# Gated delta layer of an eight-layer kernel: one table set for the norm, repeated identity products, and a new order around the key products

## The reference, cut to what matters

```
err = einsum('bhij,bhj->bhi', S, kt) - vt
S = at[..., None] * S - bt[..., None, None] * (err[..., None] * kt[:, :, None, :])
o = einsum('bhij,bhj->bhi', S, qt)
```

## Time and profile before

| | us |
|---|---|
| median of 3 runs | 2849.22 |
| lowest, highest | 2838.45, 2849.55 |
| the profiled execution's own time | 2847.4 |
| its span | 2845.6 |
| busy VectorE (DVE) | 2072.3 (73%) |
| busy ScalarE (ACT) | 1626.4 (57%) |
| busy TensorE products (PE), weight loads (PEld) | 2388.4 (84%), 1591.6 (56%) |
| mean granted TensorE clock, share of 2.4 GHz | 0.923 |

### The profile page before, as it was taken

How to read it: one execution, slowest core, us unless ns; L and a number is a source line. 1 busy time by engine, 2 the same in 40 slices (tenths; PEclk the granted TensorE clock), 3 DMA queues, 4 the chain that set the end, 5 groups by cost and what they waited for, 6 DMA issues and landing times. The chain is left out here.

```text
span 2845.6 us, 63751 instructions
## 1 busy us (share of the span) xinstructions
PE 2388.4 (84%) x25649; PEld 1591.6 (56%) x25701; DVE 2072.3 (73%) x3811; ACT 1626.4 (57%) x4119; POOL 263.7 (9%) x278
## 2 busy tenths in 40 slices
PE   6788888877888788887994999999997886999777
PEld 5666666666667666664442666666642322332376
DVE  6889998889889889882123777778726775886465
ACT  3656677666666766665234777777641113667344
POOL 0000000000000000000011101100002342110342
PEclk9889999889999989998996999999998998999889
DMA  5110111111011111002006999999510003231422
GB/s 185 32 32 17 32 32 32 32 32 30 19 32 32 32 32 30 19 17 71 0 12 173 236 249 227 232 241 233 127 37 0 0 0 103 54 88 24 172 71 65
DMA packets 205726, 219.48 MB, mean 77 GB/s; under 512 B 32966, under 2 KB 191446, under 8 KB 199990
## 3 DMA queue, kind: packets, MB, share of 16 engines
q1 hardware_dynamic: 203033, 210.44, 28.3%
q0 software_dynamic: 2400, 4.95, 0.5%
HBM read 137.96 MB, written 79.79 MB: 77 GB/s over the span
## 5 line engine op out<-in xcount | busy, mean ns | idle before, releaser
L2871 DVE TENSOR_REDUCE dl_ZO<-dl_XP 128x64 f32<-128x128 f32 (+6 forms) x448 | 219.7, 490 | 15.5
L1990 ACT ACTIVATE da_AB<-ps 128x384 f32<-128x384 f32 x256 | 124.7, 491 | 140.8 <-PE ps L1851 137.1
L2866 DVE TENSOR_TENSOR dl_XP<-dl_ZO,dl_G 128x128 f32<-128x128 f32 (+5 forms) x384 | 177.0, 461 | 13.2
L2000 ACT ACTIVATE da_E<-ps,da_top 128x512 f32<-128x512 f32 x256 | 176.2, 688 | 17.2 <-DVE da_top L2146 16.7
L2143 DVE TENSOR_TENSOR ps<-ps,da_window 128x192 f32<-128x192 f32 (+1 forms) x256 | 101.3, 396 | 116.3 <-PE ps L1874 112.0
L1470 DVE TENSOR_REDUCE ra_top<-ps 128x1 f32<-128x512 f32 x256 | 159.2, 680 | 36.2 <-PE ps L1236 22.8
L2146 DVE TENSOR_REDUCE da_top<-ps 128x1 f32<-128x512 f32 x256 | 176.9, 691 | 8.8
L2450 PE MATMUL ps<-dl_ST,ident 128*128 128x512 f32 x256 | 139.3, 672 | 46.0 <-ACT dl_Q L2638 46.0
L1370 ACT ACTIVATE ra_PT<-ps 128x512 f32<-128x512 f32 x256 | 136.0, 601 | 61.0 <-PE ps L1267 59.1
L1881 PE MATMUL ps<-ident,da_E 128*128 128x128 f32 x1024 | 168.7, 288 | 1.6 <-ACT da_E L2000 1.5
L2384 PEld LDWEIGHTS ps<-X,dl_taps_v 128*128 128x128 f32 x1088 | 145.5, 216 | 18.2 <-issue 12.9
(11 more groups left out here) (411 smaller groups left out, 5855.9 us busy)
## 6 DMA issues: line engine op xcount, KB each, us to landing
da_bands<-da_AB SPq DMA_DIRECT2D x128, 384.0 KB, 3.8
dl_Abc<-dl_ends SPq DMA_DIRECT2D x64, 512.0 KB, 6.2
da_window<-da_bands SPq DMA_DIRECT2D x128, 192.0 KB, 4.4
da_across<-da_bands SPq DMA_DIRECT2D x128, 192.0 KB, 4.5
da_parts<-da_split SPq DMA_DIRECT2D x64, 96.0 KB, 3.4
ra_parts<-ra_split SPq DMA_DIRECT2D x16, 384.0 KB, 3.5
rf_We<-in_rf_We SPq DMA_DIRECT2D x1, 4608.0 KB, 24.1
da_K<-da_parts SPq DMA_DIRECT2D x16, 256.0 KB
```

The lines of the kernel that those rows point to most:

```text
L1990: eng.activation(AB[:, j % STAGES, h, :, :], ps[:, band_bank(v), 0:2 * BAND].rearrange("p (k x) -> p k x", k=2), ACT.Copy)\
L2000: eng.activation(E[:, U % 2, :], ps[:, score_bank(U), :], ACT.Exp, bias=top[:, u:u + 1], accum_out=total[:, m % 2, u:u + 1]).then_inc(s["e ...
L2866: link(eng.tensor_tensor(XP[:, :, :, SB - t:], seen.unsqueeze(1).to_broadcast([P, 2, I, t + 1]), G[:, x:x + 2, keys][:, ::-1, :].unsqueeze ...
L2871: link(eng.tensor_reduce(ZO[:, to:to + 1 + (2 * I - 1) * CH:CH].rearrange("p (k i) -> p k i", k=2), XP[:, :, :, SB - 1 - t:], AXX, ALU.add))
```

## The change

Four edits, all in `delta_attention`:

1. ScalarE's `deviation` loads the set with both Ln and Exp by name before it waits for the variance, and the third eviction of pass n+1 goes behind it.
2. TensorE multiplies quarter 2 with the identity five times more, right before `kept(2)`, into the same bank with start and stop set, so that the following `kept(2)` overwrites it.
3. In `boundary(n, 1)` the last key products go behind the updates, and on VectorE `prepare(n + 1, 1)` goes ahead of `gate_keys(n + 1)` and the residual.
4. ScalarE's `lay_values(n + 1, 1)` is cut in two: steps 0 to 3, then the copy of the later products, then steps 4 to 15.

```diff
+    REPEATS = 5
...
-            def kept(r):
-                eng.matmul(ps[:, UPDATES[r], :], c.ident[:, :], quarters[:, r, :, :], start=True, stop=False)
+            def kept(r, alone=False):
+                eng.matmul(ps[:, UPDATES[r], :], c.ident[:, :], quarters[:, r, :, :], start=True, stop=alone)
...
                 eng.sem_inc(c.past, 1)
+                for g, k, h, r in itertools.product(range(GR), range(2), range(2), range(GR)):
+                    update(g, k, h, r)
                 if e == 1:
                     key_products(LAST_KEYS).then_inc(s["g"], 1)
-                for g, k, h, r in itertools.product(range(GR), range(2), range(2), range(GR)):
-                    update(g, k, h, r)
...
                 eng.wait_ge(s["evac"], (n + 1) * PROJ + 3)
+                for _ in range(REPEATS):
+                    kept(2, True)
                 kept(2)
...
             def deviation(n):
+                eng.preload_act_table_set("natural_log_exp_and_others")
                 eng.wait_ge(s["var"], n + 1)
...
-            def lay_values(m, e):
+            def lay_values(m, e, first=0, last=CH):
...
-                for t in range(CH):
+                for t in range(first, last):
                     ins = eng.activation(bv[:, e, :, t], values[:, t, :], ACT.Copy, scale=beta_now[:, 0, t:t + 1])
-                ins.then_inc(s["laid"], 1)
+                if last == CH:
+                    ins.then_inc(s["laid"], 1)
...
-                evacuate(n + 1, 1, 3)
+                evacuate(n + 1, 1, 2)
                 if not first:
                     deviation(n - 1)
+                evacuate(n + 1, 2, 3)
...
-                lay_values(n + 1, 1)
+                lay_values(n + 1, 1, 0, 4)
                 later_products(n + 1)
+                lay_values(n + 1, 1, 4)
                 scale_decays(n + 1, 1)
...
                 end(n, 1, first)
+                prepare(n + 1, 1)
                 gate_keys(n + 1)
                 if not first:
                     residual(n - 1)
-                prepare(n + 1, 1)
                 begin(n + 1, 0)
```

## The result

| | before | after |
|---|---|---|
| median, us | 2850.22 (6 runs) | 2863.73 (6 runs, 2859.57 to 2868.29) |
| profiled execution, its span | 2847.4, 2845.6 | 2868.29, 2866.5 |
| busy VectorE | 2072.3 | 2072.8 |
| busy ScalarE | 1626.4 | 1583.3 |
| busy TensorE products | 2388.4 | 2426.2 |

The kernel before was measured again beside the changed one. The ratio of the runs is 1.0049, with a 95% interval of 1.0030 to 1.0068: the changed kernel is 14 us slower. The forecast was 2865. The time was forecast well, but two of its terms were off in opposite directions, so part of the agreement is luck; the steps are taken one by one further down.

What follows compares the result with a forecast made beforehand. VectorE was taken to bound the stage, through its waits before L2803 (new starts) and L2831 (cross products). +6 for the first two edits and +12 for the last two made +18 on 2847.4, so 2865 us, range 2826 to 2882.

Steps and rivals of the forecast that it cites:

- What bounds the kernel: VectorE sets the stage's period, standing still before L2803 for new starts (67.0 us) and L2831 for cross products (12.6 us).
- (a): TensorE no longer waits at L2450 for the logarithm, which follows the variance product directly, with one table load before it.
- (b): In first halves TensorE runs 18 kept-product records in a row (8.1 us), with transposes some 2 us behind W.
- (c): VectorE's wait for new starts before L2803 in second halves is under 1 us in most passes.
- (d): ScalarE stands idle 2 to 4 us before L2612, the copy of the later products.
- (e): VectorE's wait for cross products before L2831 is near 3 us a pass, some 45 us in all, against 12.6.
- +6: First and second edit, us over 15 passes: per pass -3.07 for the wait, +4.5 for repeats, -0.9 for the clock.
- +12: Third and fourth edit together, us: VectorE's waits at L2803 and L2831 go from 2.9 to 3.65 a pass, times 16.
- Rival 1: Later products come early as TensorE's issue stalls fall elsewhere, clock as forecast: -19, 2828 us; chance 0.17.
- Rival 2: TensorE is granted 2.4 GHz through first halves, second halves as forecast: -6, 2841 us; chance 0.15.
- Rival 3: Gate keys come late, so VectorE waits before L2747, and repeats run partly at 1.2 GHz: 2881 us; chance 0.10.
- Rival 4: The wait before L2803 shrinks by what L2831's grows, and repeats fill idle time: 2849 us; chance 0.14.

Runs made afterwards that it cites:

- norm_rep: The kernel before with only the first and second edit: 2859.88 us against 2865.28 for the kernel before, ratio 0.9990.
- nosplit: The changed kernel with the fourth edit undone, all 16 value scalings ahead of the later products' copy: 2825.99 us against 2852.01 for the kernel before, ratio 0.9913.
- split_only: The kernel before with the fourth edit alone: 2904.57 us against 2865.95 for the kernel before, ratio 1.0133.
- split12: The whole change, but twelve value scalings ahead of the later products' copy and four behind: 2847.13 us against 2868.03 for the kernel before, ratio 0.9922.
- rep3: The changed kernel without its fourth edit and with three repeated identity products, not five: 2819.47 us against 2865.28 for the kernel before, ratio 0.9853.
- rep1: The changed kernel without its fourth edit and with one repeated identity product, not five: 2822.82 us against 2865.28 for the kernel before, ratio 0.9863.
- rep2: The changed kernel without its fourth edit and with two repeated identity products, not five: 2821.92 us against 2865.95 for the kernel before, ratio 0.9852.

## Right or wrong, step by step

- **What bounds the kernel** held throughout. Every experiment's mark follows VectorE's idle time, most of it in the two waits and, where the third edit is in, in a third, for the gate keys. That the granted clock "dips in every slice" was read too strongly off the page, whose 9 means 90% or more; it is true of the slices of this stage (0.85 to 0.93).
- **(a) The logarithm**: right. No wait at L2450, one load, at 615.75, and the logarithm right behind the variance product. The aside on what the loads are worth counted one load where its own text has two a pass: by the rows the edit frees 2 x 1.28 = 2.6 us of ScalarE and not 1.3 (31 loads and 43 us in all), and by the price quoted it would be 5.3 and not 2.7. The sum does not use it.
- **(b) 18 records**: 7.89 us for the 8.1 forecast, transposes 1.83 us behind W on the mean ("some 2 us").
- **(c) The wait before L2803 in second halves under 1 us**: 0.53 on the mean, at most 1.26.
- **(d) ScalarE idle 2 to 4 us before L2612**: 3.9 on the mean (58.9 in 15), in single passes up to 5.1.
- **(e) Some 45 us before L2831**: 44.8.
- **The size of the first and second edit failed.** "+6" was forecast. By the ratio they gave -3 us (-8 to +3), and -12 by the mark of one execution. Two things were mis-sized. The kept products: "-3.07 +4.5 -0.9" is +0.5 a pass. The 18 records took 7.73 us from their first to the transposes in every one of the fifteen passes, 0.43 a record and not 0.45, and the eight with their wait had taken 7.87 on the mean: -0.14. (Of the rows of six, eight were slow and seven fast, not the other way round; by these the clock's share is -1.1.) So the transposes came 0.17 us earlier behind W than before, not later. And what stands behind them was left out: from the transposes to VectorE's L2803 it took 7.33 us before and 6.93 with norm_rep, another 0.4 us a pass. The updates and the starts took 1.88 and 3.40 us before, 1.58 and 3.28 with norm_rep, at a mean grant of 0.92 and 0.96.
- **The size of the third and fourth edit was too small.** "+12" was forecast; by the ratios (1.0049 against 0.9990) it was +17, some 8 either way, by the marks +28. So the ratios alone don't rule the 12 out; the waits speak against it. The forecast took a second half and the cross products behind it at 2.9 us before and 3.65 after. Measured, the waits are 2.19+0.24+0.60=3.03 before (0.24 is the middle of the same pass) and 0.53+0.12+2.81=3.46 after: as forecast. But the gate keys add 0.74, 4.20 in all, and so +1.17 a pass and not +0.75. The prediction saw this wait coming in "about six passes" (it was seven, 11.1 us), and said that it takes back what is won there, but it isn't in the 3.65.
- **Within that term** the copy was to come "0.7 us sooner". It came 1.07 sooner (11.85 to 10.78), and L2649 1.41 us later and not 1.95. On the other side, first halves with the split take longer. From the transposes to L2803 it is 7.34 us with the split and 6.98 without. The marks show 46 us for the fourth edit, of which the wait for cross products holds 2.19 x 16 = 35. Why TensorE takes longer there isn't settled.
- **So the sum, 2865 for 2864, was right with two terms off by some 5 to 18 us in opposite directions, and that they cancel is luck.** The decisive mechanism, twelve scalings moved behind a wait for TensorE and VectorE paying at L2831, was right and is shown by nosplit and split_only, with split12 between. The sign of the first term was wrong: the repeats were to cost more than the first edit frees, and they didn't.
- **Rival 1** (later products early): the copy did start 1.1 us sooner, but ScalarE's chain behind it had twelve scalings more. **Rival 2** (the clock holds): it did hold through the 18 records in every pass, and to the end of the boundary in eight of fifteen; in the other seven the mean grant there was 0.78 to 0.89. The variance product, on which the rival's bound rested, took 3.3 us on the mean before and after. The waits in first halves are as before (2.06 for 2.02). **Rival 3**: VectorE does wait before L2747 now, as its point had it, but for 11 us; and no repeat ran at 1.2 GHz, from which its +22 was taken. **Rival 4** had no change; the result is 0.49% above it, and the interval begins at 0.3%.
- **Not foreseen**: that three of the four edits without the last make the kernel faster by 0.9%, and with one to three repeats by 1.4 to 1.5%. Among these three the lowest median is rep3's, 2819.47 us against 2865.28, but they can't be told apart.

## What to carry to other kernels

An engine that waits is not late: work in front of its wait is free as long as it fits into the wait, and the same work moved behind the wait lengthens the chain, here by 2.4 to 2.9 us a pass for 2.65 us of work. Filler for the clock, work done only to keep TensorE busy, has a right size: it should end near the time at which the awaited tile comes. With none the engine goes on at half the rate, with too much it comes late, and both cost the same here. And a change of several edits is measured edit by edit, for its sum can be near nothing while one edit costs some 1.3% and the others bring 0.9.

## What the runs showed of the hardware

- TensorE's pauses with no releaser, 1 to 2.3 us long in its dense stretches of small products, fall 256 TensorE instructions apart or a multiple of that (20 of 21 before, 29 of 29 after): 39 more instructions a pass moved them from five wandering lines to two that alternate. An edit that adds TensorE instructions, repeats too, moves them, and a part of every small difference in the second table may be that.
- In a first half, a wait of 2.56 us for W was followed by a granted clock of 0.50 for the whole boundary, and one of 0.97 us (rep1) by 1.00. Both had busy kept products ahead of the wait. In between it goes either way: 1.60 and 1.80 us (rep1) were followed by 1.00, 1.47 and 1.74 us (rep2) by a mean of 0.63 and 0.64.
- The unchanged stages behind the mark took 1531 to 1556 us in executions of different kernels on different chips, a spread of 25 us where the changed stage was to be told to within 10. A mark at the stage's end leaves this spread out.
